# Latent loop unrolled, attended heads fed to the output layer in two parts, closing work spread by tile

## The reference, cut to what matters

```python
qk = jnp.einsum('bsghd,blgd->bghsl', q, kc) * (1.0 / DQK ** 0.5)
att = jax.nn.softmax(qk, axis=-1)
z = jnp.einsum('bghsl,blgd->bsghd', att, vc).reshape(b, s, G * H * DV)
zn = _l2norm(z, G * H * DV) * wz_g1
h1 = jax.nn.silu(zn @ wz_w1 + wz_b1)
h1n = _l2norm(h1, 2 * FF) * wz_g2
out = jax.nn.silu(h1n @ wz_w2 + wz_b2)
```

## Time and profile before

| what | value |
|---|---|
| median of 3 runs | 3522.86 us (3520.49 to 3529.72) |
| the profiled execution's own time | 3516.9 us |
| its span in the trace | 3514.9 us |
| PE busy | 3193.8 us, 91% |
| DVE busy | 2432.3 us, 69% |
| ACT busy | 1703.7 us, 48% |
| POOL busy | 1507.9 us, 43% |
| mean granted TensorE clock | 0.959 of full |

### The profile page before, as it was taken

One profiled execution on the slowest core, in us unless ns is written; L12 is line 12 of the kernel. 1 busy time (PEld: TensorE's weight loads), 2 busy tenths in 40 slices (PEclk: granted clock), 3 DMA queues, 4 the chain that ended last, 5 costly groups with the idle time before them and its releaser, 6 DMA issues.

```text
span 3514.9 us, 58244 instructions
## 1 busy us (share of the span) xinstructions
PE 3193.8 (91%) x19248; PEld 2700.9 (77%) x19248; DVE 2432.3 (69%) x4411; ACT 1703.7 (48%) x2906; POOL 1507.9 (43%) x1399
## 2 busy tenths in 40 slices
PE   1599799777999999879999999999799999999997
PEld 1355455467888888769888988898789999999996
DVE  1467667644766767667777777777577777777774
ACT  0344344333665656425445544554455555555554
POOL 5411111001100000226666666666466666666663
PEclk9899999979999999989999999999899999999997
DMA  1100000000000000100000100000000000000000
GB/s 40 42 0 0 0 1 0 0 25 33 1 0 0 0 0 0 43 28 28 28 22 26 35 21 28 28 28 28 19 28 27 27 27 27 27 27 27 27 33 6
DMA packets 29103, 69.04 MB, mean 20 GB/s; under 512 B 5581, under 2 KB 9813, under 8 KB 28217
## 3 DMA queue, kind: packets, MB, share of 16 engines
q1 hardware_dynamic: 27448, 64.16, 5.3%
q0 software_dynamic: 1536, 3.15, 0.3%
HBM read 66.25 MB, written 1.05 MB: 19 GB/s over the span
## 4 chain that ended last, share of the span: by engine, by line
PE 47%; issue 5%; POOL 3%; DVE 1%; ACT 0%; POOLq 0%; DVEq 0%; ACTq 0%
PE lat_ps_h L1821 19%; PE lat_ps_z L1835 9%; PE lat_ps_s L1747 7%; PE lat_ps_t L1774 6%; PE lat_ps_z L1765 3%; POOL lat_zz L1554 2%; PE lat_ps_z L1757 2%; PE lat_ps_z L1845 1%; POOL latm_wq L1533 0%; POOL latm_wq L1527 0%; PE lat_ps_s L1863 0%; POOL latm_att L1546 0%; POOL latm_vcg L1538 0%; DVE latm_top L1593 0%; DVE latm_tot L1603 0%
## 5 line engine op out<-in xcount | busy, mean ns | idle before, releaser
L1821 PE MATMUL lat_ps_h<-latm_share,latm_attT 100*128 100x256 f32 x6144 | 893.0, 288 | 5.9 <-issue 5.4
L1821 PEld LDWEIGHTS lat_ps_h<-latm_share,latm_attT 100*128 100x128 f32 x6144 | 825.0, 190 | 30.9 <-DVE latm_attT L1610 10.7
L1546 POOL TENSOR_TENSOR latm_att<-latm_sc,latm_tot 128x400 f32<-128x400 f32 x516 | 440.6, 854 | 647.7 <-DVE latm_tot L1605 620.5
L1554 POOL TENSOR_TENSOR lat_zz<-lat_zz,lat_zsq 128x512 f32<-128x512 f32 x514 | 659.2, 1282 | 0.3
L1682 ACT ACTIVATE latm_sc<-latm_sc 128x400 f32<-128x400 f32 x516 | 278.3, 539 | 439.6 <-DVE latm_sc L1596 439.6
L1835 PE MATMUL lat_ps_z<-latm_attT,latm_vg 100*128 100x512 f32 x1536 | 489.9, 427 | 0.0
L1610 DVE TENSOR_TENSOR latm_attT<-lat_ps_t,latm_attT 100x512 fp32r<-100x512 f32 x514 | 349.9, 681 | 74.3 <-ACT latm_attT L1698 74.3
L1603 DVE TENSOR_REDUCE latm_tot<-latm_sc 128x4 f32<-128x400 f32 x516 | 291.3, 564 | 157.0 <-ACT latm_sc L1682 157.0
L1747 PE MATMUL lat_ps_s<-latm_wk,lat_xr 128*128 128x400 f32 x1548 | 371.0, 348 | 12.2 <-issue 12.2
L1698 ACT CAST latm_attT<-lat_ps_t 100x512 fp32r<-100x512 f32 x514 | 300.4, 584 | 163.6 <-PE lat_ps_t L1774 139.2
L1747 PEld LDWEIGHTS lat_ps_s<-latm_wk,lat_xr 128*128 128x128 f32 x1548 | 291.3, 191 | 61.2 <-issue 15.4
(11 more groups left out here) (352 smaller groups left out, 4728.3 us busy)
## 6 DMA issues: line engine op xcount, KB each, us to landing
lat_w_in<-in_w_quads SPq DMA_DIRECT2D x65, 512.0 KB, 3.5
lat_wq_in<-in_wq_quads SPq DMA_DIRECT2D x65, 256.0 KB, 2.7
moe_w<-in_W SPq DMA_DIRECT2D x2, 1024.0 KB
mha_wqk<-in_Wqk SPq DMA_DIRECT2D x1, 1152.0 KB, 5.1
ret_xpos<-in_xpos_q SPq DMA_DIRECT2D x1, 1024.0 KB, 5.5
ret_xpos<-in_xpos_k SPq DMA_DIRECT2D x1, 1024.0 KB, 4.7
latw_wkv<-in_Wkv SPq DMA_DIRECT2D x1, 1024.0 KB
out<-latm_res SPq DMA_DIRECT2D x2, 512.0 KB, 3.9
```

The costliest lines, as they stand in the source:

```text
L1546: nc.gpsimd.tensor_tensor(att[:, u].rearrange("p (j l) -> p j l", j=QH), sc[:, u].rearrange("p (j l) -> p j l", j=QH), tot[:, u].unsqueeze ...
L1554: nc.gpsimd.tensor_tensor(zz[:, t], zz[:, t], zsq[:, u], ALU.add).then_inc(s["zz_added"], 1)
L1821: mm = e.matmul(ps_h[:, t, :], attT[:, t % 2, a_part, j * P:(j + 1) * P], share[:, u, w_part, j * FF2:(j + 1) * FF2], start=False, stop=Fa ...
```

## The change

What it does:

- **No share.** z is kept: ACT copies ps_z rounded (`high_z`), DVE subtracts for the low part (`low_z`) into zr, and 12 matmuls of zr with the split quad of g1 x wz_w1 (`w1p`, 128 rows x 256) add to ps_h, one turn later than z was made. w1p is made once per quad without PE: POOL scales two halves (`scale_w1`, t = 4, 5), ACT rounds them (`high_w1`, t = 5, 6), DVE takes the low parts (`low_w1`, t = 6, 7). vcT and its computation, vcg and vg go.
- **z is read three times** from the one bank: `high_z`, `low_z`, then the square, which now waits for `low_z`. `free_z` holds the next writer of ps_z for the square and `low_z`; `add` waits for `z_high` and, before its last four matmuls, for `z_low`.
- **The subtraction of the maxima goes to ACT**: four exponentials of 100 columns with the negated maximum as bias, read from ps_s, in place of one of 400 and DVE's L1596.
- **No hardware loop**: all 512 turns are written out on each engine; both batches are one run of turns.
- **Tails by tile.** `closing` gives each tile's steps a turn. Norm, affine step, tanh (SiLU is made from tanh), and a Newton inverse root of 15 small DVE instructions for each group of 4 tiles replace the batch-wide steps and ACT's square roots; tiles of batch 0 are closed during batch 1, at t = 5 and 7 of a quad.

```diff
-            share = m2.sb("share", [L, 2, 2, QH * FF2], F32R)
-            vcg = m2.sb("vcg", [P, 2, QH, L])
+            w1s = m2.sb("w1s", [P, 2, BANK])
+            w1p = m2.sb("w1p", [P, 2, 2, QH * FF2], F32R)
...
+            def closing(i):
+                e = last_of(i)
+                full = last_of(i // GROUP * GROUP + GROUP - 1)
+                pair = i % GROUP // 2
+                if i < TB:
+                    base = NS + TB + TB * i
+                    return {"norm": e + 3 + (i == 0), "affine": full + 4, "tanh": full + 4, "gate": full + 6, "square": full + 6, "power": full + 7,
+                            "turn": base + 5, "result": base + 7, "out_tanh": base + 7, "out": base + 8}
+                return {"norm": e + 3, "affine": full + 3, "tanh": full + 3, "gate": full + 4, "square": full + 4, "power": full + 5,
+                        "turn": full + 6 + pair, "result": full + 7 + pair, "out_tanh": full + 7 + pair, "out": full + 8 + pair}
...
+                def scale_w1(q, half):
+                    e.wait_ge(w1_loaded[q % 2], 16 * (q // 2 + 1))
+                    e.wait_ge(s["w1_ready"], START + max(0, 2 * q + half - 1))
+                    nc.gpsimd.tensor_tensor(w1s[:, half].rearrange("p (j f) -> p j f", j=2), w1_in[:, q % 2, 2 * half:2 * half + 2],
+                                            g1[:, q % NQ, 2 * half:2 * half + 2].unsqueeze(2).to_broadcast([P, 2, FF2]),
+                                            ALU.mult).then_inc(s["w1_scaled"], 1)
...
-                    e.wait_ge(s["weighted"], START + free)
-                    e.tensor_tensor(sc[:, u].rearrange("p (j l) -> p j l", j=QH), src,
-                                    top[:, u].unsqueeze(2).to_broadcast([P, QH, L]), ALU.subtract).then_inc(s["shifted"], 1)
...
+                def maxima(n):
+                    e.wait_ge(s["scores_ready"], START + n + 1)
+                    e.tensor_reduce(top[:, n % 2], ps_s[:, n % 2, 0:HL].rearrange("p (j l) -> p j l", j=QH), AX.X, ALU.max,
+                                    negate=True).then_inc(s["topped"], 1)
...
+                def low_z(n):
+                    u = n % 2
+                    e.wait_ge(s["z_high"], START + n + 1)
+                    e.tensor_tensor(zr[:, u, 1], ps_z[:], zr[:, u, 0].bitcast(F32), ALU.subtract).then_inc(s["z_low"], 1)
...
+                    e.wait_ge(s["w1_high"], START + 2 * q + half + 1)
+                    e.tensor_tensor(w1p[:, q % 2, 1, cols], w1s[:, half], w1p[:, q % 2, 0, cols].bitcast(F32),
+                                    ALU.subtract).then_inc(s["w1_ready"], 1)
...
+                def inverse_root(which, i, floor, done):
+                    x, y = (a[:, which, i:i + GROUP] for a in (sums, inv))
+                    c.then(e.tensor_scalar(x, x, floor, None, ALU.max))
+                    c.then(e.tensor_scalar(y.bitcast(I32), x.bitcast(I32), 1, None, ALU.logical_shift_right))
+                    c.then(e.tensor_scalar(y.bitcast(I32), y.bitcast(I32), -1.0, float(0x5f3759df), ALU.mult, ALU.add))
+                    for n in range(3):
+                        c.then(e.tensor_tensor(newton[:], y, y, ALU.mult))
+                        c.then(e.tensor_tensor(newton[:], newton[:], x, ALU.mult))
+                        c.then(e.tensor_scalar(newton[:], newton[:], -0.5, 1.5, ALU.mult, ALU.add))
+                        c.then(e.tensor_tensor(y, y, newton[:], ALU.mult))
...
+                for n in range(END):
+                    q, t = quad(n), n % TB
+                    next_quad = q + 1 < B * NQ
+                    if 1 <= n <= K:
+                        low_z(n - 1)
+                    if n + 2 < K:
+                        maxima(n + 2)
+                    if t == 3 and next_quad:
+                        low_wk(q + 1)
+                    for i in due(n, "norm"):
+                        norm(i)
+                    for i in due(n, "result"):
+                        project(i)
+                    if 1 <= n < K:
+                        low(n)
+                    if n + 2 < K:
+                        total(n + 2)
+                    if next_quad:
+                        if t == 1:
+                            mean_wq(q + 1)
+                        if t in (6, 7):
+                            low_w1(q + 1, t - 6)
...
+                    for i in due(n, "affine"):
+                        if i % GROUP == 0:
+                            e.wait_ge(s["norm_kept"], START + i + GROUP)
+                            inverse_root(0, i, 1e-24 / (G * GH * D), "norm_inverted")
+                        affine(i)
...
...
+                def exponentials(n):
+                    u = n % 2
+                    e.wait_ge(s["topped"], START + n + 1)
+                    e.wait_ge(s["weighted"], START + max(0, n - 1))
+                    for j in range(QH):
+                        last = e.activation(sc[:, u, j * L:(j + 1) * L], ps_s[:, u, j * L:(j + 1) * L], ACT.Exp, bias=top[:, u, j:j + 1])
+                    last.then_inc(s["exped"], 1)
...
+                def high_z(n):
+                    e.wait_ge(s["z_ready"], START + n + 1)
+                    e.wait_ge(s["added"], START + max(0, n - 1))
+                    e.copy(zr[:, n % 2, 0], ps_z[:]).then_inc(s["z_high"], 1)
...
+                    e.wait_ge(s["z_low"], START + n + 1)
+                    e.activation(dst, ps_z[:], ACT.Square).then_inc(s["squared"], 1)
...
+                    if t == 3 and next_quad:
+                        high_wk(q + 1)
+                    for i in due(n, "turn"):
+                        keep_h1T(i)
+                    if n + 2 < K:
+                        exponentials(n + 2)
+                    if n < K:
+                        high_z(n)
+                    if n + 1 < K:
+                        high(n + 1)
+                    if n < K:
+                        square(n)
+                    if t in (5, 6) and next_quad:
+                        high_w1(q + 1, t - 5)
...
+                def free_z(n):
+                    e.wait_ge(s["squared"], START + n)
+                    e.wait_ge(s["z_low"], START + n)
...
+                    e.wait_ge(s["z_high"], START + n + 1)
+                    for z_part, w_part in PARTS:
+                        if z_part == 1:
+                            e.wait_ge(s["z_low"], START + n + 1)
                         for j in range(QH):
+                            if (z_part, w_part, j) == (0, 0, 3):
+                                between()
+                            first = fresh and t % 2 == 0 and (z_part, w_part, j) == (0, 0, 0)
+                            last = n % NS >= NS - TB and (z_part, w_part, j) == (1, 0, QH - 1)
+                            mm = e.matmul(ps_h[:, t, :], zr[:, u, z_part, j * P:(j + 1) * P], w1p[:, q % 2, w_part, j * FF2:(j + 1) * FF2],
+                                          start=first, stop=last, skip_group_check=True)
...
+                def reduce_heads(n):
+                    row = n // NS * G + n % NS // (4 * TB)
+                    u = n % 2
+                    e.wait_ge(s["attT_ready"], START + n + 1)
+                    for i, (v_part, a_part) in enumerate(PARTS):
+                        mm = e.matmul(ps_z[:], vc[:, v_part, row], attT[:, u, a_part], start=(i == 0), stop=(i == 2))
+                    mm.then_inc(s["z_ready"], 1)
...
+                    def between():
+                        if t == 3 and q + 1 < B * NQ:
+                            free_z(n)
+                            make_wk(q + 1)
+                        for i in due(n, "norm"):
+                            free_z(min(n, K))
+                            e.wait_ge(s["norm_kept"], START + i)
+                            norm_z(i)
...
+                    if n + 2 < K:
+                        score(n + 2)
+                    if 1 <= n <= K:
+                        add(n - 1, between)
+                    else:
+                        between()
...
+                    if n < K:
+                        if n >= 1:
+                            free_z(n)
+                        if t == 3 and q + 1 < B * NQ:
+                            e.wait_ge(s["wk_ready"], START + q + 2)
+                        for i in due(n, "norm"):
+                            e.wait_ge(s["norm_kept"], START + i + 1)
...
+                        reduce_heads(n)
+                    if n + 1 < K:
+                        turn(n + 1)
```

583 lines of the change are left out of this document (266 added, 317 removed).

## The result

| | before | after |
|---|---|---|
| median | 3521.95 us (4 runs, 3520.49 to 3529.72) | 3757.81 us (4 runs, 3754.17 to 3761.47) |
| ratio | | 1.0662, 95% interval 1.0645 to 1.0680 |
| the profiled execution's own time, span | 3516.9, 3514.9 us | 3759.7, 3757.9 us |
| PE, DVE, ACT busy (share of span) | 91%, 69%, 48% | 85%, 65%, 58% |
| mean granted clock | 0.959 | 0.963 |

What follows compares the result with a forecast made beforehand. PE bounded the kernel before; after the change z's cycle through ACT and DVE would. Quads +160, jumps -38, work before the loop -3 and -4, tails +4 make +119 us: 3642 us predicted, range 3550 to 3750.

Steps and rivals of the forecast that it cites:

- the turn with the mean: At t = 1, mean_wq behind the sum in DVE's queue makes the next low_z some 0.6 us late.
- the jumps: Writing out the hardware loop removes its jumps back, seven of them costly in batch 0: -38 us.
- the cycle: From z to next z: ACT's high_z, DVE's low_z, maxima and low part of attT, then PE; 3.41 us a turn.
- Rival 1: PE stays the pace and the cycle hides: a quad 26.0 us, 3322 us in all; chance 15%.
- rival 4: The written-out straight code starves an engine of instructions; no size given; chance 2%.
- Rival 3: PE's idling in the wk turn (t = 3) lowers its clock: about 2 us a quad, +128, 3770 us; chance 6%.
- So a plain turn lasts 3.41 us: A turn without extra quad work lasts 3.41 us, not PE's own 3.11.
- 3 x 0.16 + 0.28 = 0.76 us: ACT's four exponentials of 128 x 100 from PSUM take 0.76 us, hidden in a plain turn.
- 0.3 late, twice: At t = 5 and 6, high_w1 delays the exponentials and low_w1 precedes low_z: 0.3 us late in each.
- rival 2: The four small exponentials don't overlap, 1.12 us; 1.4 us a quad over four turns, +90, 3732 us; chance 12%.
- Now its writer waits for the square: At t = 3, wk's write to ps_z waits for the square; that turn lasts 2.5 us over a plain one.
- Closing batch 0's tiles in batch 1 ... 2.4 us a tile, 19: h1's transposes and the result each go in ps_z behind a square: 2.4 us a tile, 19 us.

Runs made afterwards that it cites:

- E5: The changed kernel without low_z, the last four adds reading the rounded z a second time: 3537.93 us, ratio 1.0047 to the kernel before.
- E3: The changed kernel with DVE's low part of attT put ahead of the maxima: ratio 1.1043 to the kernel before.
- E12: E11 with the change's four exponentials of 100 columns put back: 3600.42 us, ratio 1.0204 to the kernel before.
- E4: The changed kernel with the edits of E2 and E3 together: ratio 1.0419 to the kernel before.
- E1: The kernel before with its five loops over g written out, nothing else: 3451.71 us, ratio 0.9872.
- E6: The changed kernel with SyncE's load of the quad after next ahead of the closed tile's stores: 3735.16 us, ratio 1.0597 to the kernel before.
- E2: The changed kernel with one maximum over four heads and one exponential of 400 columns instead of four of 100: ratio 1.0381 to the kernel before.
- E9: The changed kernel with only POOL's centring of wq moved ahead of the weighting: 3739.37 us, ratio 1.0605 to the kernel before.
- E7: E4 with the wq, wk and w1 steps on POOL, DVE and ACT reordered by need: 3502.86 us, ratio 0.9946 to the kernel before.
- E11: E10 with the second half of batch 0's closing work put off to the end: 3419.17 us, ratio 0.9697 to the kernel before.
- E10: E7 with E6's loads ahead of stores, and w1's low parts on POOL instead of DVE: 3441.54 us, ratio 0.9762 to the kernel before.
- E8: E1's kernel with negated maxima and four exponentials from PSUM replacing DVE's subtraction and one exponential: 3459.8 us, ratio 0.9819 to the kernel before.

## Why the prediction was right or wrong

The direction and the mechanism were right, and sizes in the sum were wrong. The quad was forecast at +2.5 us over before and is at +4.1: 0.10 too little on each of eight turns (51 us over 64 quads), 0.34 too little on two turns for the exponentials (44), 0.28 too little on the turn with wk (18), and 0.11 too much on the turn with the mean (7). Closing work adds 17 us to the miss and the stretch ahead of the first z 5; the jumps take 2 back.

*Right, and shown:* the cycle. Its order, its links and that the low part of attT is what PE waits for are in the timeline; E5 takes one link out, and the turn falls with the same matmuls. E3 and E12 show that a second way, through the exponentials, lies close to it (3.55 us in their order of the queues), and E4 shortens both. Rival 1 (PE stays the pace) is out by the windows, rival 4 by E1, in which straight code alone gave evenly 28.5. Rival 3 (the clock falls) is out for the plain turns and the turns with wk of batch 0, by the clock of 0.99. In batch 1 the clock did fall, in the quads that store a tile, behind waits of another kind (E6). The sign for PE's busy share, below 85%, did not come: it is 87% and 85% in the two loops.

*The jumps* (-38) were right: E1. By the Trainium skill, page "Runtime: NRT & Kernel Launch", section "Instruction fetch mechanics", a taken branch to code outside the fetched window stalls the engine. E1 agrees with this in batch 0, 39.7 us for seven jumps; in batch 1 as many jumps cost 4.3 us.

*Wrong: "So a plain turn lasts 3.41 us"*. 3.50. The rows give low_z to maxima 0.60 (0.58 taken), the low part 0.68 (0.66), rounding 0.59 (0.58), and from the low part's end to PE's load 0.12 (0.06). Some 0.10 in all, 51 us over 512 turns. The bound of 0.05 a turn in the forecast was too narrow, and more than half of the miss is one hand-over time, from DVE to PE, that was taken too short.

*Wrong: "3 x 0.16 + 0.28 = 0.76 us"* for the exponentials, *and "0.3 late, twice"*. They take 1.04: 352 ns for one, the starts 0.23 apart. In a plain turn that is hidden, as said. Behind w1's rounding they end when z ends, and low_z starts 0.63 late. These turns are 0.64 over a plain one, 0.34 more than forecast, twice a quad: 44 us. So rival 2's size was nearly right (1.12). E2 prices it: with one exponential a quad falls by 1.6 us, 104 us over 64 quads. Of this, the two turns with w1's roundings give 0.46 each (from 4.15 to 3.69), the turn with the mean 0.46 and the turn with wk 0.24: the four turns that rival 2 named. It asked 1.4 us a quad on top of the forecast; the forecast had some of it already, under other names. Its range held rival 2 alone, but not together with the longer plain turns.

By the Trainium skill, page "VectorE: DVE Perf Modes", section "The TRN2 errata — SBUF-src ops pay a fixed extra latency per instruction", a ScalarE instruction from PSUM takes 172 cycles and one per element at 1.2 GHz; for 100 elements this is an estimate of 0.227 us. The trace agrees with it as the spacing of the starts (0.23) and not as the duration of one (0.352), so that four take 1.04 us and not the 0.91 that the prediction worked out. (Those 0.91 lie 0.15 of the 0.36 us, two fifths and not a third, of the way to rival 2.)

*Wrong: "Now its writer waits for the square"*. It waits for POOL too. The forecast did not follow POOL's centring of wq, which comes late because the weighting ahead of it waits for the sum. This is 0.24 us (E9), 15 us in all, of the 0.28 by which this turn's surplus (2.78 over a plain one) was missed.

*Right by luck: the turn with the mean*, 4.0. Its delay was taken for `mean_wq`; E2 shows that it is mostly the sum, late by the exponentials, since with one exponential the turn is 3.54.

*Wrong: "Closing batch 0's tiles in batch 1 ... 2.4 us a tile, 19"*. The nine quads of batch 1 behind its first took 37 us in all over 32.6 each. 19 of them come from SyncE's queue, store ahead of load, which the prediction did not look at (E6, the lower clock with it). Without it a closed tile costs 34.9 - 32.6 = 2.3 us, as priced. The first half of batch 0's closing work, in the quads on both sides of the batches' border, took 46.9 + 56.4 - 2 x 32.6 = 38 us where 16 + 13 + 4 = 33 were priced. The end was nearly as forecast: the last four norm turns and the root's turn take 12 us over plain ones for 10, and 34.0 us follow from the start of the last z on. All in all +21 for +4, inside its bounds.

The range failed since three terms of the quad erred the same way. They were not independent: E2 changes the exponentials alone, and both the turns with w1's roundings and the turn with wk fall.

*The turn with wk in E7 to E11*, 5.8 to 6.0 us for the 5.35 of E7's expectation, is in the traces. In E7 the rounding of z ends at 2127.25 but low_z starts at 2127.60, held by `mean_wq` and the sum behind it, which now stand ahead of it: 0.31 us over a hand-over of 0.04. In E10 and E11 this is 0.50. And z's load starts 0.23 us behind wk's low part, where it is 0.12 behind attT's. Together these are 0.42 and 0.61 us. No run moved `mean_wq` elsewhere.

*Still open:* the price of the 15-instruction roots was not tried by itself, nor a kernel that keeps the shares and has E11's closing work and one exponential. So how much of E11's gain over E8 the new feeding of the output layer brings is not shown.

## What to carry to other kernels

When one PSUM bank gets more readers, write down the loop from its writer back to its writer through every engine's program order, and do it anew for each kind of turn that has extra work: there another way through the same queues can be the longest. Moving one instruction to the front of a queue moves the wait to what it passed: E3 was slower than the change, and with one exponential as well the same order reached PE's pace, though only in the plain turns. For each store or load put in a shared queue, ask what it waits for and which load stands behind it.

## What was not expected of the hardware

- DVE's subtraction of two SBUF operands (128 x 512) and POOL's addition of the same size slow each other, and the later one pays. DVE's took 1.37 us for 0.69 where POOL's had begun 0.46 us earlier, and POOL's took 1.76 us for 1.29 where DVE's had begun 0.08 us earlier (E7's rows). In the change POOL's weighting took 1.21 us for 0.85 behind such a subtraction. With one operand in PSUM, DVE's subtractions (low_z, attT's low part) kept their 0.66 to 0.69 in all turns.
- Exponentials of 128 x 100 from PSUM with a bias start 0.23 us apart, where copies and activations of 128 x 128 in the earlier trace rows start 0.14 to 0.18 apart. Whether it is the bias that makes the difference was not tried.
- The 14 jumps back of the kernel before cost 39.7 us in batch 0 and 4.3 in batch 1 (E1), with the same code in both; why was not tried.
- Behind waits of PE of 1.57 to 2.49 us the granted clock fell to the lower level for 3.4 or 6.8 us in five of eight quads (E6's rows); behind the waits ahead of wk in batch 0, 1.03 us in the one looked at, it stayed at 1.00.
